# Shifting the low-rank folds by two products, and a residual load by one place in the DMA queue, in the last stage of a fused transformer block

## The reference, cut to what matters

```python
out = jnp.einsum('bsd,hd->bsh', x, w)
out = out + jnp.einsum('bsr,hr->bsh', jnp.einsum('bsd,rd->bsr', x, a), b) * scale   # _matmul_lora
...
hidden = jax.nn.silu(gate) * up                                    # 1024 tokens x 2752
out = _matmul_lora(hidden, down_w, down_a, down_b)                 # 1024 tokens x 1024
...
x = x + _L1_ffn_ref(_layernorm(x, axis=-1), ...)
```

## Time and profile before

| | |
|---|---|
| median of 3 runs | 1175.09 us (1174.22 to 1178.73) |
| profiled execution, its own time | 1178.73 us |
| its span, first to last instruction | 1176.9 us |
| TensorE busy | 1087.5 us |
| VectorE busy | 919.6 us |
| mean granted TensorE clock | 0.979 |

### The profile page before, as it was taken

One profiled execution on the slowest core, in us unless ns is written; L12 is line 12 of the kernel. 1 busy time (PEld: TensorE's weight loads), 2 busy tenths in 40 slices (PEclk: granted clock), 3 DMA queues, 4 the chain that ended last, 5 costly groups with the idle time before them and its releaser, 6 DMA issues.

```text
span 1176.9 us, 16329 instructions
## 1 busy us (share of the span) xinstructions
PE 1087.5 (92%) x6034; PEld 531.5 (45%) x6034; DVE 919.6 (78%) x1830; ACT 524.3 (45%) x815; POOL 155.6 (13%) x183
## 2 busy tenths in 40 slices
PE   4786999899989999969999999999999988989988
PEld 2353554644445444424444444444444433444443
DVE  8999988888994187977988888887878857474755
ACT  6896753772144225755444454444443432121211
POOL 4883340082004010000000000000000000000000
PEclk9997999999999999999999999999999999998989
DMA  9720000123032038963335334343111722223211
GB/s 366 266 96 1 2 1 1 72 84 96 1 107 86 0 87 218 220 131 97 99 90 171 90 125 134 109 121 112 64 62 36 268 81 81 90 73 98 71 64 54
DMA packets 104207, 118.44 MB, mean 101 GB/s; under 512 B 74752, under 2 KB 78976, under 8 KB 104128
## 3 DMA queue, kind: packets, MB, share of 16 engines
q1 hardware_dynamic: 104128, 117.40, 32.3%
HBM read 86.97 MB, written 16.78 MB: 88 GB/s over the span
## 4 chain that ended last, share of the span: by engine, by line
PE 69%; DVE 23%; ACT 3%; issue 3%; DMA 1%; SPq 0%; DVEq 0%; ACTq 0%
PE PAIR L2789 31%; PE PAIR L2887 14%; PE PAIR L2441 6%; PE PAIR L2442 6%; PE PAIR L2443 6%; DVE X L1734 2%; DVE PAIR L1686 2%; PE PAIR L2744 2%; DVE LORA L1685 1%; DVE LORA L1687 1%; DVE POOL L1867 1%; DVE T4B L2001 1%; DVE POOL L1560 1%; DVE BST L1532 1%; DVE BST L1533 1%
## 5 line engine op out<-in xcount | busy, mean ns | idle before, releaser
L2789 PE MATMUL PAIR<-XT,POOL 128*128 128x512 f16 x1008 | 230.2, 382 | 10.6 <-DMA XT<-POOL 6.8
L2789 PEld LDWEIGHTS PAIR<-XT,POOL 128*128 128x128 f16 x1008 | 98.1, 98 | 127.1 <-issue 14.0
L1129 ACT ACTIVATE POOL<-STG 128x512 f16<-128x512 f32 (+1 forms) x167 | 96.2, 612 | 89.5 <-DVE STG L1975 84.8
L2887 PE MATMUL PAIR<-POOL 128*128 128x512 f16 x528 | 127.9, 394 | 2.8 <-DVE POOL L1867 2.8
L2441 PE MATMUL PAIR<-POOL 128*128 128x512 f16 x336 | 128.3, 382 | 2.3 <-DVE POOL L1777 2.3
L2442 PE MATMUL PAIR<-POOL 128*128 128x512 f16 x336 | 128.5, 382 | 0.0
L2443 PE MATMUL PAIR<-POOL 128*128 128x512 f16 x336 | 128.4, 382 | 0.0
L2789 PE MATMUL PAIR<-X,POOL 128*128 128x512 f16 x504 | 115.7, 379 | 0.4 <-DMA X<-POOL 0.4
L1129 ACT ACTIVATE POOL<-ST 128x512 f16<-128x512 f32 (+1 forms) x64 | 39.5, 617 | 169.4 <-DVE ST L1862 169.4
L1867 DVE TENSOR_TENSOR POOL<-STG,POOL 128x512 f16<-128x512 f32 (+1 forms) x167 | 106.3, 669 | 1.2 <-ACT POOL L1129 1.1
L1975 DVE SCALAR_TENSOR_TENSOR STG<-STG,PAIR 128x512 f32<-128x512 f32 (+1 forms) x48 | 30.8, 642 | 78.6 <-PE PAIR L2821 78.6
(11 more groups left out here) (342 smaller groups left out, 1945.9 us busy)
## 6 DMA issues: line engine op xcount, KB each, us to landing
STG<-in_gate_w SPq DMA_DIRECT2D x21, 512.0 KB, 5.0
STG<-in_up_w SPq DMA_DIRECT2D x21, 512.0 KB, 5.6
STG<-in_ctx_t SPq DMA_DIRECT2D x16, 512.0 KB, 4.1
STG<-in_ctx SPq DMA_DIRECT2D x16, 512.0 KB, 4.2
STG<-in_down_w SPq DMA_DIRECT2D x16, 512.0 KB, 4.8
POOL<-in_ctx SPq DMA_DIRECT2D x12, 512.0 KB, 10.9
X<-in_x SPq DMA_DIRECT2D x8, 512.0 KB, 9.7
xt_keep<-POOL SPq DMA_DIRECT2D x16, 256.0 KB, 3.0
```

The costliest lines, as they stand in the source:

```text
L1129: e.activation(block(j, name)[:, 0, :, :], src, ACT.Copy).then_inc(b_hi, 1)
L2789: i = e.matmul(dst, blk[:, a_, k, :], src[:, b_, k, :], start=(opens and k == 0 and n == 0), stop=(k == KD // 2 - 1 and n == 2), skip_grou ...
L2887: last = e.matmul(dst, blk[:, a_, i - i0, :], src[:, b_, :], start=first, stop=(c == NSET - 1 and i == i1 - 1 and n == 2))
```

## The change

In `send`'s loop the third and fourth residual load of a pass are issued one chunk earlier in the order: behind the weight loads of chunk 3p+2 instead of those of chunk 3p+3. In pass 3 there is only chunk 11, and the order there stays. On TensorE the folds of the next chunk stand after S1, S2, S4 and S3 of chunks 1 to 10, instead of after A11, A12, S1 and S2. In chunk 0 they stay after S2, S4, S3 and A22.

```diff
@@ sync @@
                 for d in range(NSET * p + 2, min(NSET * p + 5, CHUNKS)):
                     load_down(2 * d)
                     load_down(2 * d + 1)
-                    if d == min(NSET * p + 3, CHUNKS - 1):
+                    if d == NSET * p + 2:
                         load_sum(p, 2)
                         load_sum(p, 3)
                 send(p)
@@ tensor @@
             for j in range(HT, HT + CHUNKS):
-                first = 3 if j == HT else 0
+                first = 3 if j == HT else 2
                 for n, name in enumerate(BLOCKS):
                     down_product(j, name)
                     if j + 1 < HT + CHUNKS and first <= n < first + 4:
                         down_fold(j + 1, n - first)
```

## The result

The changed kernel takes 1185.76 us (median of 4 runs, 1184.68 to 1187.55), the kernel before 1174.65 us beside it (4 runs, 1172.8 to 1178.73). The ratio is 1.0091, 95% interval 1.0062 to 1.012: **slower by 0.9%, some 11 us**. The forecast was 1182.3 us in 1175 to 1189. One execution of a later run, gated_loads, took 1646.78 us at a granted clock of 0.65 and is in no comparison.

A forecast was written before the change was run, and what follows sets the result against it. TensorE, busy for 92% of the span, was taken as the bound, so only its idle time or clock counts. Idle time -2.7 - 3.3 + 9.8 = +3.8 us and clock +3.4 give +7.2 on 1175.1: 1182.3 us, range 1175 to 1189.

The forecast's parts named there:

- Step (a): Chunk 1: with the first fold after S1, no fold waits for a `down_add` any more, -2.7 us.
- Step (b): Chunks 3, 6, 9: S1 follows A12 without a fold between, so the wait there goes, 3 x -5.0 us.
- Step (c): Ahead of A11 of chunks 3, 6, 9: idle time grows from 1.1 to 5.0 us, 3 x +3.9 us.
- Step (d): Between chunks of one pass: a late last fold costs nothing, as A22 and A11 cover at least 4.5 us.
- The residual loads: Issued no sooner, they delay chunk 3p+3's weight loads; its second fold waits 3.3 us, three times, +9.8 us.
- T + 7.95: Issue time of chunk 3p+3's load; T is the start of the product behind chunk 3p+2's last fold.
- the landing: Chunk 3p+3's weight load lands 5.1 us after its issue; bounds 3.4 and 6.5 us.
- the clock behind the new waits: Slow products behind the three new waits: 1.7 us at two of three, +3.4 us; bounds 0 and 7.5.
- rival 2: Every new wait costs clock: +8.9 to +11.3 us, 1184 to 1186 us, up to 1191 with slow landings; chance 0.24.
- the likeliest case: The forecast itself, with two clock losses at the three new waits: 1180 to 1184 us; chance 0.38.
- The clock at the 5.0 us waits: Slow products behind the one 5.0 us wait per pass: 6.6 us in all, carried over unchanged.
- The rival on the other side: Rival 3: loads come in time, the second fold never waits; only the folds' shift counts, -6.0, 1169.1 us; chance 0.06.

The follow-up runs named there:

- gated_loads: The changed kernel with the two loads of chunk 3p+4 held back until the first half of chunk 3p+3 has landed and been added; 1186.01 us.
- folds_only: The kernel before with the later folds alone, in the old order of the loads; 1168.82 us against 1176.05, ratio 0.994.
- late_at_pass_end: The kernel before with the folds shifted only in chunks 2, 5, 8; 1183.94 us, ratio 1.0067.
- Filled_wait: The changed kernel with 18 extra matmuls of zeros between S2 and the second fold in chunks 2, 5, 8; 1182.61 us against 1186.46 for the changed kernel.
- loads_only: The kernel before with the new order of the loads alone, folds where they stood; 1189.92 us, ratio 1.0116.

## Why the prediction came out

**Right, by its own steps.** Step (a): chunk 1 has no wait. Step (b): A12 is followed by S1, 15 us of waits are gone. Step (c): the wait ahead of A11 is 5.0 us to a tenth, and folds_only and late_at_pass_end put it down to the folds in chunks 2, 5, 8. Step (d): no other chunk waits. The residual loads: the issue is where the forecast had it, T + 7.95 (967.05 and 975.00), because VectorE's first sum ends its wait, and the weight loads stand behind it.

**Mis-sized: the landing.** I took 5.1 us, the median of all 20 weight loads of the stage. The place's own three read 4.9, 6.5 and 5.1 in the trace before; over all traces it is 6.1 to 6.3, and in the changed kernel's trace 6.9, 6.8 and 5.9. So the new waits came to 14.0 us in place of 9.8, the upper bound that the prediction gave for them. The fit of 3.2 us that it cites from the Trainium skill ("DMA: Bandwidth & Descriptors", Anatomy of one DMA) was farther off still. The page gives that fit for DMAs issued by GpSimd, and SyncE issues these.

**Mis-sized: the clock behind the new waits.** 6.0 us in place of 3.4; the forecast let one of the three waits pass at full clock, and all three fell. That is rival 2, and 1185.8 us lies in its range of 1184 to 1186, above the 1180 to 1184 of the likeliest case, though with slower landings than that range took. One number of that rival is wrong: between the two waits of a pass lie not 4.6 but 6.5 us of work (three products of 1.94 us, three folds of 0.23). No term used it. Filled_wait gave back 3.85 us of it by measured time. The clock at the 5.0 us waits, carried over as 6.6, was 5.9.

**The sum, and some luck.** The idle time is +8.0 us (-2.7 - 3.3 + 14.0) where the forecast had +3.8, and the clock at the new waits +6.0 where it had +3.4. That makes +14.0, less 1.1 at the old waits: +12.9, as the +12.8 us from chunk 1 on confirm. Put on 1175.1 us, it is 1188, just inside the range. What the trace lost less ahead of chunk 1, 2.7 us, no step foresaw, and it differs from execution to execution: it brings the account to 10.2 us against a span that grew by 10.1, and with it near the median's +11.1. So the mechanism and the direction came out by the forecast's own steps, and both large terms were too small. Why the medians grew less (+11.1 and +12.3 us) than the stretch from chunk 1 on did in the two traces (+12.8 and +14.8) stays open.

The rival on the other side, the loads in time, is not how the kernel went, but it named the part worth keeping: folds_only is 7.2 us faster where that rival had 6.0.

## What to carry to other kernels

A transfer that waits in an in-order queue is not sooner for being put further ahead; what it does is to hold back everything put behind it, here weights that were due 15 us earlier. A shift that removes a stall at one place of a repeated pattern can put it back at another: look at each place of the pattern and shift it by itself (here one formula for all chunks gave -7 us and one for each chunk of a pass -22 to -28 us). For a landing time, read the same place of the queue in several traces, not the median of the stage.

## What the runs showed of the hardware

- Whether a short stand of TensorE costs clock is not told by its length. The 2.1 us wait in chunk 0 cost 1.7 us in the trace before and nothing in the one after (1.6 to 1.7 us in five of twelve traces, nothing in seven); a wait of 2.7 us in chunk 1 cost nothing in the kernel before, and one of 2.9 us in chunk 5 of loads_only some 1.7 us. Each wait of 4 us and more that was not filled, in the traces before and after, was followed by a stretch at a granted clock of 0.50.
- A slow stretch that ends in a wait for another engine is free: in late_at_pass_end 1.7 us of it shortened the next wait from 5.0 to 3.3 us.
- The same 512 KB load at the same place of the queue lands after anything from 4.5 to 7.8 us.
